# Output projection and ternary network of a two-layer block, made one stage

## The chip, the cores and the metric

The kernel is one program on one core of a Trainium2 chip. Times are device microseconds (us). An execution's time is a little longer than the span that its profile shows, by what lies around the span.

The engines are TensorE (PE in the profile, its weight loads PEld), VectorE (DVE), ScalarE (ACT), GpSimd (POOL) and SyncE (SP), which issues the DMAs. Each runs its own list of instructions in order; between lists only semaphores order the work. PEclk is the TensorE clock that was granted, as a share of its upper level.

## The reference

The input x has 8 x 256 rows of 512 values. Two layers run over it, each an attention and a feed-forward network. The change touches what follows the attention of the second layer: its output projection, and the network with ternary weights.

```python
# L1_xattn, its end: 16 heads of 32, attention weights rounded to 1/255 of each row's largest
out = jnp.einsum('bhqk,bhkd->bhqd', attn, v)
return out @ Wp + bp                      # Wp [512, 512]
...
# L1_ffn
def _bit_quant(w):
    scale = jnp.maximum(jnp.mean(jnp.abs(w)), EPS)
    return jnp.clip(jnp.round(w / scale), -1.0, 1.0)   # the value that is used
w1q = _bit_quant(w1)                      # [2048, 512]
w2q = _bit_quant(w2)                      # [512, 2048]
h = jnp.einsum('bsd,fd->bsf', x, w1q) + b1
h = jax.nn.gelu(h, approximate=False)
return jnp.einsum('bsf,df->bsd', h, w2q) + b2
...
x = x + _L1_xattn_ref(_layernorm(x), ctx, Wq, bq, Wkv, bkv, Wp, bp)
x = x + _L1_ffn_ref(_layernorm(x), w1, b1, w2, b2)
```

The mean of the absolute weights runs over a whole matrix, so no weight can be made ternary before all of its matrix has been read.

## The kernel before

x stays on the chip as 16 tiles of 128 rows (`x_sb`, NT = 16). The program is a row of stages, each a block in which every engine has its list; no engine passes the end of a stage before all have reached it. The stages are: the attention and the gated network of the first layer, keys, values, queries, `attend`, `project` and `ternary_ffn`. The last three matter here.

`attend` goes through 256 units (16 tiles by 16 heads). For each, TensorE makes the scores, ScalarE their exponentials as bytes (L1571), a DMA on SyncE's queue turns the bytes (`a_pairs`, L1443), GpSimd widens them (L1550), and TensorE weighs the values into `a_psO`, which VectorE keeps in `QO` (L1513).

`project` works by tile. VectorE divides by the sum of the exponentials (`p_o`, L1621); TensorE turns the tile (`p_psX`, L1685); ScalarE scales it (`p_oT`, L1659); TensorE multiplies it by Wp in four-byte floats (`p_psY`, L1692); VectorE adds the bias (L1628) and the product (L1633) to x and takes the tile's statistics (L1636). Wp and bp are fetched at the stage's start, and behind them on the same queue w1 and w2 (4 MB each, into `KT`, which the attention no longer needs). In the second half of the stage ScalarE sums the absolute values of w1 and w2, one of 16 pieces at a time (L1669). At the end VectorE works out the normalisation for all 16 tiles (L110 to L112 and a chain of small operations).

`ternary_ffn` first makes w1 ternary as a whole, on VectorE, in three operations of 128 x 8192 (L1785 to L1787). Then it goes through four chunks of 512 rows (NTC = 4, TPC = 4 tiles in each). A chunk is two passes on TensorE. The up pass makes 16 groups (FC = 16) of 128 hidden values by 512 rows: eight products each of 128 x 512, since x is held as two half-precision parts, hi and lo (`t_psH`, L1869). The down pass follows when the whole hidden layer of the chunk is there: per tile 32 products into one bank (`t_psY`, L1881). Between the passes TensorE turns the next chunk's rows (`t_psX`, L1860). ScalarE applies gelu (L1845); VectorE splits its result into hi (L1804) and lo (L1806). In the first chunk VectorE also makes one group of w2 ternary ahead of each split (L1785 to L1787, now 128 x 512). `t_psH` has two buffers and `t_h` two.

There is no scheduler: each engine's order is written out by hand, and chunks 1 and 2 run in a loop of registers.

## Time and profile before

| what | value |
|---|---|
| three runs, median (lowest to highest) | 1968.65 us (1966.84 to 1968.81) |
| the profiled execution | 1971.55 us, of it 1969.8 us span |
| busy, share of the span | PE 89%, DVE 80%, ACT 62%, POOL 47% |
| mean granted clock | 0.958 |
| the attention's last VectorE copy | starts at 1614.71 |
| the first up product of the ternary network | starts at 1714.01 |
| the last addition to x | starts at 1966.41 |

The shares are means over stages with different limits, so the table doesn't say what an edit in one stage is worth. For that the views of the stretch from 1614 us to the end are read: what each engine did, what it waited for, and which wait ended last. A product of 128 x 512 shows a duration of 0.38 us, but the next one starts 0.216 us later: products overlap, and what counts is the distance between their starts. The same holds, less strongly, for VectorE: 0.68 us operations that don't depend on each other start 0.60 us apart.

### The profile page before, as it was taken

To read this page: it belongs to the slowest core of one execution; us is meant where nothing else is said; L and a number is where in the kernel's file an instruction comes from. 1 tells how busy PE (TensorE), PEld (TensorE's weight loads), DVE (VectorE), ACT (ScalarE), POOL (GpSimd) and SP (SyncE) were. 2 spreads that over 40 slices of the span, in tenths; PEclk is the share of its full clock that TensorE was granted. 3 is DMA by queue.
4 is the path that set the end of the run, shared out by engine and by line. 5 is a ranking of instruction groups with operands and counts; after the bars stand their busy time and mean duration, and the time that the engine had idled before them with its cause. 6 is when DMAs were issued, how large, how long until landed. Compare 5 with 4: busy or idle time off the path is not lost. (4 is left out here: it accounts for less than half of the span.)

```text
span 1969.8 us, 32510 instructions
## 1 busy us (share of the span) xinstructions
PE 1760.5 (89%) x11262; PEld 786.4 (40%) x11262; DVE 1584.5 (80%) x2930; ACT 1230.8 (62%) x2011; POOL 918.7 (47%) x935
## 2 busy tenths in 40 slices
PE   4999989599999969939899999999999969579998
PEld 1322322144444435425344444444444434234443
DVE  5899999776776678868899999999999956774433
ACT  4888876455454324414599999999999965222111
POOL 6576764464544300020188888888888850000000
PEclk8999999799999989959899999999999989799999
DMA  9764640300000021000054555555565553000000
GB/s 210 205 163 108 160 119 12 110 11 11 22 0 22 0 80 34 24 27 0 16 108 108 108 108 107 109 106 110 103 109 108 108 131 142 6 6 17 22 22 22
DMA packets 334720, 147.54 MB, mean 75 GB/s; under 512 B 290544, under 2 KB 306928, under 8 KB 333424
## 3 DMA queue, kind: packets, MB, share of 16 engines
q1 hardware_dynamic: 334576, 145.70, 31.8%
q8 instruction: 81, 1.33, 0.3%
q14 instruction: 63, 0.52, 0.1%
HBM read 70.15 MB, written 4.19 MB: 38 GB/s over the span
## 5 line engine op out<-in xcount | busy, mean ns | idle before, releaser
L1571 ACT ACTIVATE a_prob<-a_psS,a_bias,q_scale 128x1024 uint8<-128x1024 f32 x512 | 610.2, 1211 | 28.3 <-PE a_psS L1464 24.4
L1500 DVE TENSOR_REDUCE a_tops<-a_psM 128x1 f32<-128x512 f32 x1024 | 622.6, 677 | 2.2 <-PE a_psM L1454 0.8
L1550 POOL CAST a_wide<-a_pairs 128x2048 int16<-128x2048 uint8 x256 | 481.4, 1891 | 99.5 <-DMA a_pairs<-a_prob 84.8
L1454 PE MATMUL a_psM<-KT,QO 128*128 128x512 bf16 x1024 | 370.7, 387 | 5.6 <-PEq L1248 2.2
L1464 PE MATMUL a_psS<-KT,QO 128*128 128x512 bf16 x1024 | 305.4, 380 | 4.3 <-ACT a_prob L1571 4.3
L1476 PEld LDWEIGHTS a_psO<-V,a_wide 128*128 128x128 f16 x4096 | 175.1, 96 | 146.4 <-DVE QO L1513 23.0
L1476 PE MATMUL a_psO<-V,a_wide 128*128 128x32 bf16 x4096 | 181.5, 177 | 21.8 <-DVE QO L1513 15.6
L854 DVE SCALAR_TENSOR_TENSOR g_sum<-g_psG,gu_scale,g_sum 128x512 f32<-128x512 f32 x176 | 124.2, 745 | 89.7 <-PE g_psG L1006 74.9
L832 POOL TENSOR_TENSOR g_sum<-g_sum 128x512 f32<-128x512 f32 x88 | 126.3, 1436 | 140.4 <-DVE g_sum L854 140.4
L489 ACT ACTIVATE prob<-psT 128x512 f32<-128x512 f32 x256 | 142.9, 598 | 68.5 <-PE psT L698 68.1
L953 ACT ACTIVATE g_sum<-g_psG,gu_scale 128x512 f32<-128x512 f32 x176 | 111.2, 681 | 109.6 <-PE g_psG L1006 108.9
L554 DVE TENSOR_REDUCE rmax<-psS 128x1 f32<-128x512 f32 x256 | 158.6, 673 | 12.1 <-PE psS L684 10.5
L1019 PE MATMUL g_psY<-raw_dn,g_hT 128*128 128x512 f32 x352 | 163.1, 592 | 0.0
L1454 PEld LDWEIGHTS a_psM<-KT,QO 128*128 128x128 bf16 x1024 | 96.9, 96 | 137.4 <-DVE a_tops L1500 133.3
L1845 ACT ACTIVATE t_h<-t_psH,t_b 128x512 f32<-128x512 f32 x64 | 44.0, 687 | 162.3 <-PE t_psH L1869 143.5
L684 PE MATMUL psS<-ks,qs 128*128 128x512 f16 x256 | 93.1, 395 | 41.9 <-POOL qs L413 22.0
L1464 PEld LDWEIGHTS a_psS<-KT,QO 128*128 128x128 bf16 x1024 | 96.4, 98 | 68.7 <-ACT a_prob L1571 12.6
L413 POOL TENSOR_TENSOR qs<-xs,q_sub 128x512 f16<-128x512 f32 x64 | 74.8, 1191 | 87.6 <-ACT q_sub L481 83.3
L1571 ACT ACTIVATION_READ_ACCUMULATOR a_prob<-a_psS,a_bias,q_scale 128x1 f32 x512 | 105.5, 206 | 0.0
L1869 PE MATMUL t_psH<-t_xT_hi,t_w1q 128*128 128x512 f16 x256 | 98.4, 385 | 6.6 <-ACT t_h L1845 5.1
L1881 PE MATMUL t_psY<-t_w2q,t_hT_hi 128*128 128x512 f16 x256 | 99.1, 387 | 2.0 <-DVE t_hT_lo L1806 2.0
L694 PE MATMUL psT<-qs,ks 128*128 128x512 f16 x256 | 98.4, 384 | 0.9 <-ACT prob L489 0.9
(211 smaller groups left out, 2862.0 us busy)
## 6 DMA issues: line engine op xcount, KB each, us to landing
xs<-in_x SPq DMA_DIRECT2D x64, 256.0 KB, 6.5
cs<-in_ctx SPq DMA_DIRECT2D x64, 256.0 KB, 8.4
KT<-in_w SPq DMA_DIRECT2D x2, 4096.0 KB, 21.1
raw_gu<-in_gu SPq DMA_DIRECT2D x4, 1408.0 KB, 8.4
vs<-in_ctxT SPq DMA_DIRECT2D x16, 256.0 KB, 2.8
k_cT<-in_ctxT SPq DMA_DIRECT2D x16, 256.0 KB, 2.7
a_pairs<-a_prob SPq DMA_TRANSPOSE x256, 2.7
out<-x_sb SPq DMA_DIRECT2D x16, 256.0 KB, 2.0
```

The source lines that it names most:

```text
L489: act.activation(prob[:, g % RING, :], psT[g % NT3][:, :], ACT.Exp, scale=float(D0) ** -0.5).then_inc(exped, 1)
L554: v.reduce_max(rmax[j % 2][:, n:n + 1], psS[(NG * j + n) % 3][:, :], AX.X).then_inc(maxed, 1)
L832: pool.tensor_tensor(a[:, :], a[:, :], b[:, :], ALU.add).then_inc(totalled, 1)
L854: v.scalar_tensor_tensor(out=acc[:, :], in0=psG[q % CH][:, :], scalar=gu_scale[:, i * FG + p, g:g + 1], in1=acc[:, :], op0=ALU.mult, op1=A ...
L953: act.activation(part_sum[g][i][m % 3][:, :], psG[q % CH][:, :], ACT.Copy, scale=gu_scale[:, i * FG + p, g:g + 1]).then_inc(scaled, 1)
L1019: mm = pe.matmul(psY[k][:, :], hT[t % 2][:, f, k * P:(k + 1) * P], w_dn[:, f, :], start=(f == 0), stop=(f == FG - 1))
L1454: pe.matmul(psM[n % NM][:, :], QOf[:, i * P:(i + 1) * P], KTf[:, keys:keys + 512], start=True, stop=True).then_inc(shown, 1)
L1464: mm = pe.matmul(psS[g % NS][:, c * 512:(c + 1) * 512], QOf[:, i * P:(i + 1) * P], KTf[:, keys + c * 512:keys + (c + 1) * 512], start=True ...
L1476: mm = pe.matmul(psO[:, h * D1:(h + 1) * D1], wide[i % NV][:, parity, c, :].bitcast(F16), V[:, h, 2 * c + parity, :], start=(parity == 0 a ...
L1500: v.reduce_max(tops[i // JOIN % NB][:, i % JOIN, c:c + 1], psM[n % NM][:, :], AX.X).then_inc(topped, 1)
L1550: pool.tensor_copy(wide[i % NV][:, :, :, :].rearrange("p k c q -> p k (c q)"), both).then_inc(widened, 1)
L1571: act.activation(prob[i % NP][:, k * HK:(k + 1) * HK], psS[g % NS][:, :], ACT.Exp, scale=q_scale[:, i:i + 1], bias=bias[i // JOIN % NB][:, ...
```

## The change

`project` and `ternary_ffn` become one stage, `project_and_ternary`, without a register loop.

- Wp and bp are fetched during `attend`, in five DMAs on SyncE's queue between the turning DMAs of units 112, 128, 144, 160 and 176, into parts of `QO` whose queries have been used.
- The projection has four result banks (`t_psD`) instead of two, and the same order on TensorE.
- The first chunk's rows are normalised, split into hi and lo and turned during the projection. The turning, for all chunks, is done by DMA (`x_turned`) instead of by TensorE: two DMAs of 128 x 2048 per chunk.
- The sums of absolute weights start at tile 5 instead of tile 8. The totals are made at tile 11; from tile 12 VectorE scales and clips two groups of w1 per tile (`clip`, two operations), and ScalarE takes the rounding constant off (`whole`, one operation). Eight groups of w1 are made so before the first up product or beside it (AHEAD = 8); the rest, and all of w2, go group by group through the first chunk.
- In the network, the down products of a group follow three groups behind its up products (LAG = 3). Each group's down products go to all four tiles' banks, two into each. The hidden layer is held for six groups (RING = 6) instead of 16. Up results have four banks, gelu results three buffers.
- The hi part of the hidden layer is made on ScalarE (`high`), the lo part on VectorE (`split`).
- The normalisation of tiles 4 to 15 is worked out on VectorE within group 1 of the first chunk.
- The four tiles of a chunk are finished on VectorE after group 3 of the next.

```diff
@@ attend, SyncE
+            def fetch(c):
+                sp.wait_ge(o_read, CH + 1)
+                if c < CH:
+                    sp.dma_start(spare[:, c, :].bitcast(F32), wp_in[c * P:(c + 1) * P, :]).then_inc(env["wp_loaded"], 16)
+                else:
+                    sp.dma_start(spare[:, c, :].bitcast(F32),
+                                 bp_in.partition_broadcast(P)).then_inc(env["wp_loaded"], 16)
             for i in range(N):
...
+                if i % H1 == 0 and FIRST_LOAD <= i // H1 <= FIRST_LOAD + CH:
+                    fetch(i // H1 - FIRST_LOAD)
@@ project_and_ternary, VectorE
+            def clip(i, f):
+                src = raw[i][:, f]
+                v.tensor_scalar(src, src, inv[:, i:i + 1], -1.0, ALU.mult, ALU.max).then_inc(w_clipped[i], 1)
+                v.wait_ge(w_clipped[i], 2 * f + 1)
+                v.tensor_scalar(src, src, 1.0, ROUND, ALU.min, ALU.add).then_inc(w_clipped[i], 1)
...
+            for t in range(NT):
+                v.tensor_tensor(xt, xt, bp, ALU.add).then_inc(biased, 1)
+                if t + 2 < NT:
+                    divide(t + 2)
+                if t == 4:
+                    v.wait_ge(after_s, TPC)
+                    normalise_tiles(v, env, 0, TPC)
+                if t == 5:
+                    normalise(0, 0)
+                    normalise(0, 1)
+                if t == 7:
+                    for k in (0, 1):
+                        low_part(0, k)
+                        normalise(0, k + 2)
+                if t == 9:
+                    low_part(0, 2)
+                    low_part(0, 3)
+                if t == 11:
+                    v.wait_ge(w_summed, 2 * WS)
+                    v.reduce_sum(sums[:, :], ...).then_inc(summed, 1)
+                if t == 12:
+                    scales(own)
+                if t >= 12:
+                    clip(0, 2 * (t - 12))
+                    clip(0, 2 * (t - 12) + 1)
+                project(t)
+            for t in range(NTC):
+                for p in range(FC):
+                    m = FC * t + p
+                    if t == 0 and AHEAD + p < FC:
+                        clip(0, AHEAD + p)
+                    if t == 0:
+                        clip(1, p)
+                    if m == 1:
+                        v.wait_ge(after_s, NT)
+                        normalise_tiles(v, env, TPC, NT)
+                    split(m)
+                    if t and p == LAG:
+                        for k in range(TPC):
+                            finish(t - 1, k)
...
+            for k in range(TPC):
+                finish(NTC - 1, k)
@@ ScalarE
+            for t in range(NT):
+                scaled(t)
+                if 5 <= t < 5 + WS:
+                    sum_part(2 * (t - 5))
+                    sum_part(2 * (t - 5) + 1)
+                if t == 8:
+                    high_part(0, 0)
+                    high_part(0, 1)
+                if t == 10:
+                    high_part(0, 2)
+                    high_part(0, 3)
+                if t >= 14:
+                    whole(0, 2 * (t - 14))
+                    whole(0, 2 * (t - 14) + 1)
+            for f in range(4, AHEAD):
+                whole(0, f)
+            for t in range(NTC):
+                for p in range(FC):
+                    gelu(m)
+                    high(m)
+                    if t == 0 and AHEAD + p < FC:
+                        whole(0, AHEAD + p)
+                    if t == 0:
+                        whole(1, p)
@@ TensorE
+            def up(t, p):
+                if p == 0:
+                    pe.wait_ge(x_turned[t % 2], 32 * (t // 2 + 1))
+                if t == 0:
+                    pe.wait_ge(w_ready[0], p + 1)
...
+            def down(g):
+                pe.wait_ge(h_split, g + 1)
+                for k in range(TPC):
+                    if f == 0:
+                        pe.wait_ge(added, NT + TPC * (t - 1) + k + 1)
+                    for s in range(2):
+                        mm = pe.matmul(psD[k][:, :], hT[s][:, g % RING, k * P:(k + 1) * P], w2q(f), ...)
+            def due(m):
+                if m % FC == LAG and m > FC:
+                    return []
+                if m % FC == LAG + 1 and m > FC:
+                    return [m - LAG - 1, m - LAG]
+                return [m - LAG] if m >= LAG else []
```

So at each later chunk, TensorE does no down products after up group 3 and those of two groups after up group 4.

**VectorE in the first chunk.** Before, each group of w2 takes three operations, then come the hi and lo parts of the hidden group (`t_h0` is gelu's result):

```order
L1785 TENSOR_SCALAR KT<-KT,t_inv 128x512
L1786 TENSOR_SCALAR KT<-KT 128x512
L1787 TENSOR_SCALAR t_w2q<-KT 128x512
L1804 CAST t_hT_hi<-t_h0 128x512
L1806 TENSOR_TENSOR t_hT_lo<-t_h0,t_hT_hi 128x512
L1769 TENSOR_SCALAR t_xn0<-x_sb,x_mv,x_rstd 128x512
L1769 TENSOR_SCALAR t_xn1<-x_sb,x_mv,x_rstd 128x512
```

After, `KT` with 4x128 is a group of w1, `KT` with 512 one of w2, and `t_hT_lo` the split:

```order
L1738 TENSOR_SCALAR KT<-KT,t_inv 128x4x128
L1740 TENSOR_SCALAR KT<-KT 128x4x128
L1738 TENSOR_SCALAR KT<-KT,t_inv 128x512
L1740 TENSOR_SCALAR KT<-KT 128x512
L1744 TENSOR_TENSOR t_hT_lo<-t_h0,t_hT_hi 128x512
L1738 TENSOR_SCALAR KT<-KT,t_inv 128x4x128
L1740 TENSOR_SCALAR KT<-KT 128x4x128
L1738 TENSOR_SCALAR KT<-KT,t_inv 128x512
L1740 TENSOR_SCALAR KT<-KT 128x512
L111 BN_AGGR x_mv<-x_stats 128x2 x12
L113 TENSOR_SCALAR norm_ve<-x_mv 128x12
```

Two of five operations of a group have gone to ScalarE, one more group of w1 has come in, and the normalisation of twelve tiles stands ahead of the second split.

**VectorE in the projection.** Before, from the addition of one tile's product (`p_psY0`) to that of the next, a turn is four operations:

```order
L1633 TENSOR_TENSOR x_sb<-x_sb,p_psY0 128x512
L1636 BN_STATS x_stats<-x_sb 128x6
L1628 TENSOR_TENSOR x_sb<-x_sb,p_bias 128x512
L1621 TENSOR_TENSOR p_o1<-QO,p_inv 128x512
L1633 TENSOR_TENSOR x_sb<-x_sb,p_psY1 128x512
```

After, the turn of tile 7 (`V` holds the hi and lo parts of x, `t_h0` and `t_h1` the normalised rows):

```order
L1764 TENSOR_TENSOR x_sb<-x_sb,QO 128x512
L1706 TENSOR_TENSOR t_o1<-QO,e_sum 128x512
L1729 TENSOR_TENSOR V<-t_h0,V 128x512
L1723 TENSOR_SCALAR t_h0<-x_sb,x_mv,x_rstd 128x512
L1729 TENSOR_TENSOR V<-t_h1,V 128x512
L1723 TENSOR_SCALAR t_h1<-x_sb,x_mv,x_rstd 128x512
L1713 TENSOR_TENSOR x_sb<-x_sb,t_psD3 128x512
L1715 BN_STATS x_stats<-x_sb 128x6
```

Between the division of tile 9 and the addition of tile 7 four operations have come in.

**TensorE, from the up to the down products.** Before, at the end of the first up pass:

```order
L1869 MATMUL t_psH1<-t_xT_hi,t_w1q 128x512
L1869 MATMUL t_psH1<-t_xT_lo,t_w1q 128x512
L1860 MATMUL t_psX0<-id_f,t_xn0 128x128 x4
L1860 MATMUL t_psX1<-id_f,t_xn1 128x128 x4
L1860 MATMUL t_psX0<-id_f,t_xn2 128x128 x4
L1860 MATMUL t_psX1<-id_f,t_xn3 128x128 x4
L1881 MATMUL t_psY0<-t_w2q,t_hT_hi 128x512
L1881 MATMUL t_psY0<-t_w2q,t_hT_lo 128x512
```

After, around up group 3 of the first chunk (`QO` holds the ternary weights, `V` the turned rows):

```order
L1927 MATMUL t_psU2<-V,QO 128x512 x8
L1927 MATMUL t_psU3<-V,QO 128x512 x8
L1940 MATMUL t_psD0<-QO,t_hT_hi 128x512
L1940 MATMUL t_psD0<-QO,t_hT_lo 128x512
L1940 MATMUL t_psD1<-QO,t_hT_hi 128x512
L1940 MATMUL t_psD1<-QO,t_hT_lo 128x512
L1940 MATMUL t_psD2<-QO,t_hT_hi 128x512
L1940 MATMUL t_psD2<-QO,t_hT_lo 128x512
L1940 MATMUL t_psD3<-QO,t_hT_hi 128x512
L1940 MATMUL t_psD3<-QO,t_hT_lo 128x512
L1927 MATMUL t_psU0<-V,QO 128x512 x8
```

The turnings have left TensorE, and the down products of group 0 stand between the up products of groups 3 and 4.

## Rows read from the trace of the kernel before

**Rows 1.** Stretches of the end: busy us per engine, granted clock, DMA share.

```profile
1615.00:1623.00 8.00, 0.37 (x2) 0.38 (x3) 4.57 (x7) 0.00 (x0) 0.00 (x0) 0.50 0.73 232
...
1687.00:1714.00 27.00, 4.49 (x18) 3.65 (x19) 23.53 (x48) 3.23 (x5) 0.00 (x0) 0.58 0.03 11
1714.00:1760.00 46.00, 34.26 (x146) 15.21 (x147) 39.89 (x87) 13.25 (x21) 0.00 (x0) 0.91 0.00 1
1760.00:1967.00 207.00, 200.77 (x928) 91.62 (x926) 83.46 (x146) 37.67 (x57) 0.00 (x0) 0.98 0.05 19
```

**Rows 2.** Timeline 1614 to 1634: start, us, engine, line, what, [idle before].

```profile
1614.71 0.69 DVE L1513 COPY QO<-a_psO 128x512 f32<-128x512 f32 x1 [17.70 <-PE a_psO L1476]
...
1616.11 0.50 SPq L1610 DMA_DIRECT2D p_bias<-in_bp  x1
...
1622.63 1.97 PE L1685 MATMUL p_psX<-id_f,p_o 128*128 128x128 f32 x8 [7.95 <-DMA p_bias<-in_bp]
...
1624.97 4.34 PE L1692 MATMUL p_psY<-p_w,p_oT 128*128 128x512 f32 x8 [0.38 <-ACT p_oT L1659]
```

**Rows 3.** Timeline, VectorE adding the projection, two turns.

```profile
1652.66 0.69 DVE L1633 TENSOR_TENSOR x_sb<-x_sb,p_psY 128x512 f32 x1 [1.06 <-PE p_psY L1692]
...
1656.54 0.69 DVE L1633 TENSOR_TENSOR x_sb<-x_sb,p_psY 128x512 f32 x1 [1.06 <-PE p_psY L1692]
```

**Rows 4.** Timeline, last projection tile to first up product.

```profile
1687.07 0.69 DVE L1633 TENSOR_TENSOR x_sb<-x_sb,p_psY 128x512 f32<-128x512 f32 x1 [1.42 <-PE p_psY L1692]
...
1688.52 1.17 DVE L110 BATCH_NORM_AGGREGATE x_mv<-x_stats 128x2 f32<-128x6 f32 x16
...
1692.64 0.17 DVE L93 TENSOR_TENSOR x_rstd<-x_rstd,norm_tmp 128x16 f32<-128x16 f32 x1
...
1696.42 4.49 DVE L1785 TENSOR_SCALAR KT<-KT,t_inv 128x8192 f32<-128x8192 f32 x1
...
1714.01 0.58 PE L1869 MATMUL t_psH<-t_xT_hi,t_w1q 128*128 128x512 f16 x1 [1.50 <-DVE t_xT_lo L1793]
```

**Rows 5.** Chain that ended last, 1750 to 1970: start, us, what.

```profile
1759.73 29.22 PE t_psY L1881 x128
1788.95 27.64 PE t_psH L1869 x128
...
1820.46 27.63 PE t_psY L1881 x128
...
1966.41 0.69 DVE x_sb L1819
```

**Rows 6.** Groups by line and shape, 1615 to 1970 | busy us, mean ns.

```profile
L1806 DVE TENSOR_TENSOR t_hT_lo<-t_h,t_hT_hi 128x512 f16<-128x512 f32 x64 | 44.3, 692 | 2.2
L1845 ACT ACTIVATE t_h<-t_psH,t_b 128x512 f32<-128x512 f32 x64 | 44.0, 687 | 162.3 <-PE t_psH L1869 143.5 <-DVE t_hT_lo L1806 18.7
...
L1669 ACT ACTIVATE p_junk<-KT 128x1024 bf16 x12 | 12.8, 1064 | 1.3 <-ACT p_junk L1669 1.3
...
L1785 DVE TENSOR_SCALAR KT<-KT,t_inv 128x512 f32<-128x512 f32 x16 | 7.7, 480 | 0.0
...
L1669 ACT ACTIVATION_READ_ACCUMULATOR p_junk<-KT x12 | 2.4, 202 | 0.0
```

**Rows 7.** The same view, gated network, 480 to 700.

```profile
L941 ACT ACTIVATE g_half_hi<-g_xn 128x512 f16<-128x512 f32 x8 | 5.0, 630 | 20.8 <-DVE g_xn L844 20.8
```

**Rows 8.** Two stretches of the gated network, as rows 1.

```profile
384.00:388.00 4.00, 1.12 (x4) 0.13 (x2) 3.55 (x15) 1.66 (x3) 0.00 (x0) 0.50 0.00 0
400.00:680.00 280.00, 278.25 (x957) 121.09 (x956) 198.60 (x308) 139.37 (x245) 136.82 (x100) 1.00 0.05 12
```

**Rows 9.** DMA issues of the gated network; last, median us to landing.

```profile
g_xT_lo<-g_half_lo SPq DMA_TRANSPOSE x2, 4.1
```

**Rows 10.** The same for the whole program (part 6 of the page).

```profile
KT<-in_w SPq DMA_DIRECT2D x2, 4096.0 KB, 21.1
```

**Rows 11.** Waits in the attention: who <- whom: total us, times, longest.

```profile
ACT a_prob L1571 <- DMA a_pairs<-a_prob: 3.4, 6, 1.0
```

More of the change, by code:

```diff
@@ L1402, in attend @@
     AHEAD, LAG, JOIN = 4, 4, 2
+    FIRST_LOAD = 7
     OW = P // 2
@@ L1625, in turn, with invert @@
[L1625 to L1630 removed]
+            def invert(own, first, end):
+                part = sums_of[:, first * H1:end * H1, :]
+                own.link(v.tensor_tensor(part[:, :, 0], part[:, :, 0], part[:, :, 1], ALU.add))
+                own.link(v.tensor_scalar(part[:, :, 0], part[:, :, 0], SUBNORMAL, None, ALU.mult))
+                own.link(v.reciprocal(part[:, :, 0], part[:, :, 0]))
```

490 lines of the change are left out of this document (231 added, 259 removed).

## The prediction

> **What bounds the kernel now.** I read the stretches first. Up to 1615 us nothing is changed but five small DMAs, so the question is what TensorE does in the 355 us from there to the end. It is busy all but 6 us of the last 207, but only 4.5 of the 27 us from 1687 to 1714 and 34 of the next 46, at a granted clock of 0.58 and 0.91 [rows 1]. Then the timeline: the stage of the projection begins with TensorE and VectorE waiting for the bias, issued at 1616.11 and there at 1622.63 [rows 2]. In the projection TensorE sets the pace: VectorE's additions come 3.88 us apart and VectorE is idle for 1.06 us before each [rows 3]. After the last tile comes a chain on VectorE, normalisation, then w1 made ternary as a whole, and the first up product starts at 1714.01 [rows 4]. The first up pass goes at VectorE's pace: 39.9 us busy of 46 [rows 1]. The chain that ended last then shows TensorE alone: passes of 128 products in 27.64 us, which is 0.216 us a product, and about 3.9 us between an up and a down pass, in which the last group's gelu, its split and the turning of rows are waited for [rows 5]. So three things cost time: a start, a 27 us hole, and passes that wait for their neighbours.
>
> **The sum, in the times of the profiled execution.**
>
> Start. Wp and bp are there already. VectorE begins at about 1615.7 as before; it inverts two tiles' sums (three small operations, an estimated 0.6 us together from the 0.2 us spacing of the small chain in [rows 4]) and divides tile 0 (0.69), so TensorE starts at 1617.0. From its first turning to its first projection product it took 2.34 us [rows 2]; I keep that, and the slow clock with it (PEclk 0.50 in this stretch, [rows 1]). 1619.4 instead of 1624.97: 5.6 us won. The bounds are 4 and 7.
>
> Projection. TensorE's work is the same, 62.1 us from 1624.97 to 1687.07 [rows 2, 4]. VectorE gets more: about 3.4 us of normalisation at tile 4 (the 16-tile chain took 4.3, [rows 4], of which 1.17 falls to a quarter), four normalised tiles at 0.48 and four low parts at 0.69 [rows 6], sixteen clips at 0.48 [rows 6], 0.6 for the scales: 16.4 us, against 16 turns with 1.06 idle each [rows 3]. It just fits as a sum, but comes in lumps, and TensorE can run only about one turn ahead of the divisions. The lump at tiles 4 and 5 is 4.4 us against 2.1 of idle and a little over a microsecond of lead: about 1 us of stall. At tile 7 VectorE also waits for a high part, which stands on ScalarE's list behind tile 8's scaling and two sums (1.27 each, [rows 6]): about 2.3 us. The same at tile 9: about 1.3. The clips of tiles 12 to 15 cost 1.9 us a turn against 1.06 idle, and from tile 14 the division is gone: 1. Near 6 us lost; the bounds are 0 (the lead absorbs it) and 8. The sums start at tile 5, some 23 us after the weights are asked for, and those land in 21.1 us in the median of the two [rows 10]; w1 is the first, and w2 is needed only at tile 9. I cost that at nothing.
>
> The hole. Up group 0 needs four things: the turned rows, the first ternary group, b1 and a free bank. The low parts are ready by tile 10, the two turning DMAs land some 4.1 us after each issue [rows 9], and five tiles of 3.88 cover them; the first group's last operation is ScalarE's, at tile 14, with a turn and a half of cover. So the up products follow the last projection product: 27.0 us won (1687.07 to 1714.01, [rows 4]). Bounds 24 and 27.
>
> First chunk. Before, from 1714.01 to the next chunk's first up product at 1788.95: 74.9 us [rows 4, 5]. After: 256 products at 0.216 are 55.3 us if TensorE is never late. VectorE enters the chunk about 2.8 us after TensorE. Then, with operations of 0.48 and 0.69 [rows 6]: addition and statistics 1.4, four clips 1.9, split 0.7; then four clips 1.9, twelve tiles' normalisation 4.1 (from the 4.3 of [rows 4]), split 0.7: the second split ends about 13.5 us into the chunk. TensorE wants it after five ups and one down, 10.4 us in. A stall of 3 us, and 0.5 for the first w2 group. A stall of that size brought the clock to 0.50 in the gated network [rows 8]; an estimated 1 us for that. 59.8 us: 15.1 won; bounds 10 and 19. From group 3 on a group needs 3.46 us of TensorE, at most 4 x 0.48 + 0.69 = 2.6 of VectorE, and 0.69 + 3 x 0.63 = 2.6 of ScalarE [rows 6, 7] (`whole` isn't in the trace; I take it like the copy of [rows 7]. The ends are 0.48, like a clip, and 1.27, like a sum; at 1.27 ScalarE needs 3.9 us a group, 0.4 more than TensorE, 3 us over eight groups.) So TensorE sets the pace there.
>
> Chunks 1 to 3. Before 177.5 us (1788.95 to 1966.41, [rows 5]). After, three times 55.3, and at each chunk's group 3 a new wait: the down products of the new chunk may not touch a bank before the old tile has been added to x. Split 3 is done 0.69 + 0.63 + 0.69 us after up group 3 [rows 6, 7], the first addition 0.69 later: 2.8 us with the gaps, while up group 4 covers 1.73. That is 1.2, and each of the next three additions (0.69) is 0.27 late against a pair of products (0.43). 2.0 us per chunk; queued behind it on TensorE is everything. 171.9: 5.6 won; bounds 0 and 9.
>
> End. Four additions come after the last products instead of one; the first can start 1.3 us before TensorE ends: 0.7 lost.
>
> Attention. Five more DMAs share the queue of the turning DMAs. ScalarE waited for those DMAs only 3.4 us in 256 units [rows 11]. Such a fetch took 6.5 us behind another one [rows 2]; fully exposed, five would cost 32. The units have three buffers, so I take 0.5; bounds 0 and 32.
>
> Sum: 5.6 - 6.0 + 27.0 + 15.1 + 5.6 - 0.7 - 0.5 = 46.1 us won. The profiled execution took 1971.55; the median of the runs is 1968.65, and the difference goes over unchanged: **1968.65 - 46.1 = 1922.5, say 1922 us.**
>
> **A rule on the down products.** In the gated network TensorE goes through four up banks and four down banks in just this manner, and there it is busy 278.3 of 280 us at a clock of 1.00 [rows 8]. The Trainium skill, page "TensorE: Matmul & The Clock Gate", section "A second HAM failure mode: psum-queue depth-cycling", says that going through banks in each iteration leaves small gaps between groups, that the clock then swings between its two levels, and that throughput suffers. By that rule the network's products would not all run at 2.4 GHz; it is rival D below. The trace of the gated network speaks against it.
>
> **A rule on the clips.** A contiguous clip of 512 values took 0.48 us and a two-operand operation of that size 0.69 [rows 6]; the new view of w1 is four pieces of 128. The Trainium skill, page "VectorE: DVE Perf Modes", section "What auto-detection actually checks", says that one source in SBUF keeps the double rate when the outermost dimensions are even; by that rule 0.48 stays and rival B falls away. No trace here shows it for this view.
>
> **Rivals.**
>
> B, the pieces of w1 are slow: each of the 32 w1 operations takes 0.69. Sixteen fall on VectorE in tiles 12 to 15, where it has no idle time left, 3.4 us, and four before the second split, 0.8; the late start adds some: 5 us, 1927. For it: nothing in the trace has that shape. Against it: nothing either, but the pieces are whole.
>
> C, the lumps are absorbed: TensorE's lead is longer than the turn I give it, the 6 and 3 us of stalls go to 1 and 0, and the time is 1914. For it: VectorE's work fits into its idle time as a sum [rows 3]. Against it: the second split comes late by a count of operations.
>
> D, slower than before: stalls of a microsecond or two recur, and the clock stays down, as in the gated network's first chunk (0.50 from 384 to 388, [rows 8]). The network's 512 up and 512 down products are 221 us at the upper level; the 46 us are used up when they take 267, a mean clock of 0.83. At 0.75 they take 295: 1996. For it: the early stretch of the gated network, where VectorE was just as loaded. Against it: it recovered within 20 us.
>
> E, the fetches are felt: the turning DMAs behind them come late, and the attention is bound by a chain with little slack. At a third of the exposure, 10 us: 1933. If w2's sums were late as well, the change would not do what it says, and w1 would again be waited for; the 5 tiles of cover speak against that.
>
> **Chances.** Forecast 0.70, B 0.11, C 0.09, E 0.06, D 0.04. The forecast's own range is 1917 to 1928. The range for 8 in 10 takes in C and B and most of E's near side: 1913 to 1933. A change of under 0.2% (4 us) can't be told from none here. Faster by more than that 0.95, within it 0.01, slower 0.04.
>
> **What would show it.** Right: the first projection product at about 1619; the first up product within 2 us of the last projection product, near 1687; VectorE before TensorE in the waits of tiles 7 to 12; one stall of about 3 us at the second group of down products; three of about 2 us with the addition to x as releaser; PEclk 1.00 from 1710 on; TensorE's last product near 1919. Wrong: clips of 0.69; a mean distance of products over 0.22 us in chunks 1 to 3; ScalarE's exponentials waiting for the DMA in tiles 7 to 11; or up group 0 waiting for the turned rows.

## The result, and the profile after

| | before | after |
|---|---|---|
| median of the runs, us | 1968.62 | 1919.05 |
| lowest to highest | 1966.84 to 1968.81 | 1913.82 to 1924.04 |
| profiled execution: time, span | 1971.55, 1969.8 | 1915.59, 1913.8 |
| start of the attention's last keep | 1614.7 | 1610.5 |
| first up product | 1714.0 | 1682.0 |
| A: last keep to first up product | 99.3 | 71.5 |
| B: first up product to the end of the span | 255.8 | 231.8 |

The ratio of the times is 0.975, with a 95% interval of 0.9718 to 0.9782. The forecast was 1922 (1913 to 1933); the result is 3 us below it. A keep is VectorE's copy of an attention result into `QO`. A and B are the two parts of what was changed; together they went from 355.1 to 303.3 us. They are used for every run below, since the end of the unchanged stages ahead of them, the last keep, moves by 10 us from one profile to the next (1607.7 to 1617.8 in the table of the experiments).

The stretches of the kernel after (the columns as in [rows 1]), which answer to [rows 1]:

```profile
1615.00:1623.00 8.00, 7.56 (x19) 3.56 (x19) 4.53 (x7) 2.71 (x11) 0.00 (x0) 0.81 1.02 431
1623.00:1687.00 64.00, 60.86 (x193) 28.99 (x192) 51.97 (x108) 42.41 (x100) 0.00 (x0) 1.00 0.28 88
1687.00:1714.00 27.00, 25.72 (x120) 11.52 (x119) 24.42 (x72) 21.86 (x36) 0.00 (x0) 1.00 0.00 1
1714.00:1760.00 46.00, 44.87 (x207) 19.79 (x206) 21.80 (x41) 23.76 (x37) 0.00 (x0) 1.00 0.19 46
1760.00:1912.00 152.00, 147.55 (x679) 65.51 (x676) 50.71 (x81) 57.71 (x89) 0.00 (x0) 1.00 0.13 33
```

Where TensorE was busy 4.5 us of 27 it is now busy 25.7, and its granted clock is 1.00 in every stretch from 1623 on. All its waits for another engine in the stage (from 1612 to 1914; total, times, longest) are four groups:

```profile
PE t_psU L1901 <- DVE t_o L1706: 5.9, 4, 2.7
PE t_psD L1940 <- DVE x_sb L1755: 3.4, 3, 1.1
PE t_psD L1940 <- DVE t_hT_lo L1744: 1.3, 1, 1.3
PE t_psD L1909 <- ACT t_hT_hi L1821: 0.4, 1, 0.4
```

The first group is the start (2.7) and three stalls in the projection (0.96 at 1640.8, 1.67 at 1654.3, 0.51 at 1662.8); the second is the three chunk boundaries; the third is the second down group of the first chunk.

The timeline at the start, which answers to [rows 2]:

```profile
1610.53 0.69 DVE L1531 COPY QO<-a_psO 128x512 f32<-128x512 f32 x1 [17.16 <-PE a_psO L1494]
1611.54 0.19 DVE L1698 TENSOR_TENSOR e_sum<-e_sum 128x32 f32<-128x32 f32 x1 [0.32 <-PEq L1411]
1613.20 1.94 PE L1901 MATMUL t_psU<-id_f,t_o 128*128 128x128 f32 x8 [2.72 <-DVE t_o L1706]
1615.59 1.22 PE L1909 MATMUL t_psD<-QO,t_hT_hi 128*128 128x512 f32 x1 [0.44 <-ACT t_hT_hi L1821]
```

The first projection product comes 5.06 us behind the last keep instead of 10.26.

The timeline of TensorE where the hole was [rows 4]:

```profile
1679.46 2.74 PE L1909 MATMUL t_psD<-QO,t_hT_hi 128*128 128x512 f32 x6
1682.04 7.07 PE L1927 MATMUL t_psU<-V,QO 128*128 128x512 f16 x32
...
1690.67 1.89 PE L1927 MATMUL t_psU<-V,QO 128*128 128x512 f16 x8
1693.84 0.39 PE L1940 MATMUL t_psD<-QO,t_hT_hi 128*128 128x512 f16 x1 [1.28 <-DVE t_hT_lo L1744]
```

The last projection products run straight into 32 up products; the one stall is 1.28 us.

The timeline at a chunk boundary, and behind it two groups of the chain that ended last (they answer to [rows 5]):

```profile
1747.23 0.69 DVE L1744 TENSOR_TENSOR t_hT_lo<-t_h,t_hT_hi 128x512 f16<-128x512 f32 x1 [2.76 <-ACT t_hT_hi L1860]
1747.84 2.48 DVE L1755 TENSOR_TENSOR x_sb<-t_psD,x_sb 128x512 f32<-128x512 f32 x4
1748.67 0.38 PE L1940 MATMUL t_psD<-QO,t_hT_hi 128*128 128x512 f16 x1 [1.13 <-DVE x_sb L1755]
1749.18 0.39 PE L1940 MATMUL t_psD<-QO,t_hT_hi 128*128 128x512 f16 x1
1749.78 0.39 PE L1940 MATMUL t_psD<-QO,t_hT_hi 128*128 128x512 f16 x1
```

```profile
1748.67 4.04 PE t_psD L1940 x16
...
1805.64 4.04 PE t_psD L1940 x16
...
1862.61 4.04 PE t_psD L1940 x16
1902.90 6.92 PE t_psD L1940 x32
```

VectorE takes the split first, then the four additions 0.60 us apart; TensorE waits 1.13 us and then goes at the additions' pace. The period of a chunk is 56.97 us, so the boundary costs 1.7 us over 55.3 of products.

The operations of the stage from 1682 on, by line (x count, busy us, mean ns, idle before), beside [rows 6, 7]:

```profile
L1744 DVE TENSOR_TENSOR t_hT_lo<-t_h,t_hT_hi 128x512 f16<-128x512 f32 x64 | 44.2, 691 | 123.3 <-ACT t_hT_hi L1860 123.3
L1860 ACT ACTIVATE t_hT_hi<-t_h 128x512 f16<-128x512 f32 x64 | 40.3, 629 | 2.1
L1841 ACT ACTIVATE QO<-KT,t_less_round 128x512 f16<-128x512 f32 x26 | 17.8, 709 | 5.8 <-DVE KT L1740 5.6
L1738 DVE TENSOR_SCALAR KT<-KT,t_inv 128x512 f32<-128x512 f32 x25 | 12.0, 480 | 0.0
```

VectorE now waits 123 us for ScalarE's high parts in B. It sets nothing there but for the first groups.

### The profile page after: what moved, and what is told of

It is laid out like the page before. It is cut to its first block and busy times, and to the rows that moved or that the text cites. A ratio compares the mean times of both kernels' runs of the same rounds, so it can differ in the third digit from the quotient of the medians.

```text
span 1913.8 us, 31933 instructions
## 1 busy us (share of the span) xinstructions
PE 1724.0 (90%) x11054; PEld 775.2 (41%) x11198; DVE 1547.2 (81%) x2897; ACT 1291.2 (67%) x2107; POOL 921.4 (48%) x936
## 5 line engine op out<-in xcount | busy, mean ns | idle before, releaser
L1472 PE MATMUL a_psM<-KT,QO 128*128 128x512 bf16 x968 | 352.1, 385 | 18.3 <-DVE a_tops L1518 12.6
L1482 PE MATMUL a_psS<-KT,QO 128*128 128x512 bf16 x967 | 293.3, 380 | 6.6 <-ACT a_prob L1589 3.6
L560 DVE TENSOR_REDUCE rmax<-psS 128x1 f32<-128x512 f32 x256 | 158.9, 676 | 12.7 <-PE psS L690 10.6
L1744 DVE TENSOR_TENSOR t_hT_lo<-t_h,t_hT_hi 128x512 f16<-128x512 f32 x64 | 44.2, 691 | 123.3 <-ACT t_hT_hi L1860 123.3
L1849 ACT ACTIVATE t_h<-t_psU,t_b 128x512 f32<-128x512 f32 x64 | 43.7, 682 | 92.7 <-PE t_psU L1927 92.7
L1940 PE MATMUL t_psD<-QO,t_hT_hi 128*128 128x512 f16 x256 | 97.1, 379 | 4.7 <-DVE x_sb L1755 3.4
```

The costliest lines, as they stand in the source:

```text
L560: v.reduce_max(rmax[j % 2][:, n:n + 1], psS[(NG * j + n) % 3][:, :], AX.X).then_inc(maxed, 1)
L1472: pe.matmul(psM[n % NM][:, :], QOf[:, i * P:(i + 1) * P], KTf[:, keys:keys + 512], start=True, stop=True).then_inc(shown, 1)
L1482: mm = pe.matmul(psS[g % NS][:, c * 512:(c + 1) * 512], QOf[:, i * P:(i + 1) * P], KTf[:, keys + c * 512:keys + (c + 1) * 512], start=True ...
L1940: mm = pe.matmul(psD[k][:, :], hT[s][:, g % RING, k * P:(k + 1) * P], w2q(f), start=(f == 0 and s == 0), stop=(f == FC - 1 and s == 1))
```

## The experiments

Each row is one profile; the base is the changed kernel, profiled twice. "Against" is the sum A + B against the mean of the two, 303.8 us. The last column is measured over all runs against the kernel before.

| run | last keep | A | B | A + B | against | ratio to before, 95% |
|---|---|---|---|---|---|---|
| changed | 1610.5 | 71.5 | 231.8 | 303.3 | | 0.9750 (0.9718 to 0.9782) |
| changed, again | 1614.1 | 72.5 | 231.8 | 304.3 | | 0.9742 (0.9729 to 0.9755) |
| additions ahead | 1617.2 | 70.9 | 226.7 | 297.5 | -6.2 | 0.9707 (0.9694 to 0.9721) |
| normalisation later | 1617.8 | 71.0 | 230.3 | 301.3 | -2.5 | 0.9729 (0.9716 to 0.9742) |
| low parts later | 1609.2 | 69.6 | 231.8 | 301.4 | -2.3 | 0.9722 (0.9709 to 0.9735) |
| the three together | 1612.4 | 69.8 | 225.2 | 295.0 | -8.8 | 0.9695 (0.9669 to 0.9721) |
| Wp fetched in the stage | 1613.4 | 77.5 | 231.8 | 309.3 | +5.5 | 0.9760 (0.9744 to 0.9777) |
| x turned behind the projection | 1608.4 | 86.4 | 233.4 | 319.8 | +16.0 | 0.9816 (0.9800 to 0.9833) |
| w1 quantised behind it | 1614.8 | 74.6 | 233.0 | 307.5 | +3.8 | 0.9765 (0.9749 to 0.9781) |
| one group behind | 1607.7 | 71.2 | 235.8 | 307.0 | +3.2 | 0.9768 (0.9752 to 0.9784) |
| blocks of seven | 1611.0 | 71.1 | 233.9 | 305.0 | +1.2 | 0.9738 (0.9716 to 0.9761) |
| VectorE's share | 1617.1 | 70.9 | 236.5 | 307.4 | +3.6 | 0.9756 (0.9740 to 0.9772) |
| both of these | 1610.2 | 72.4 | 241.9 | 314.4 | +10.6 | 0.9788 (0.9772 to 0.9804) |

B is repeated to 0.1 us where nothing in it was touched (231.8 in four profiles). A is not: eight profiles with the same projection (both of the changed kernel, additions ahead, normalisation later, and the last four rows) lie between 70.9 and 72.5. All of that lies in one place, the first tile's eight projection products. These are two of the eight profiles, the changed kernel again and the additions ahead:

```profile
1619.19 5.92 PE L1909 MATMUL t_psD<-QO,t_hT_hi 128*128 128x512 f32 x8 [0.44 <-ACT t_hT_hi L1821]
```

```profile
1622.23 4.28 PE L1909 MATMUL t_psD<-QO,t_hT_hi 128*128 128x512 f32 x8 [0.44 <-ACT t_hT_hi L1821]
```

In their first 4.3 us the granted clock was 0.50 and 0.86. Without these products A is 66.6 us in each of the eight (66.59 to 66.62). So a difference in B, and one in A without the first tile, is read to a few tenths; one in A as it stands in the table only to about 2 us. Idle times of TensorE are a little short as prices: a wait also ends the overlap of two products, which start 0.216 us apart while one lasts 0.38, so it costs some 0.16 more than its idle time.

**The changed kernel again.** No edit.

> The changed kernel once more, nothing altered. It is the base for the other three runs of this group and tells where the 10 us between its own runs (1913.8 to 1924.0) come from. Theory U (the spread lies in the unchanged stages ahead): the new stage, from the last keep of the attention to the end of the span, takes 303.3 us within 1 us again, whatever the total. Rival S (it lies in the new stage, a clock that falls or waits that differ): the total and that stretch move together, by up to 10 us. Ratio to the kernel before 0.972 to 0.978 in either case.

Theory U held: 304.3 against 303.3 us, and the 1.0 is the first tile's products (5.92 against 4.90). The 10 us arise ahead of the change. In two profiles the first product of the gated network, 1250 us before the stage, is apart by 4.8 us already, first the changed kernel's, then that of the run with the normalisation later:

```profile
L1012 PE MATMUL g_psG<-first_xT_hi,w_gu x176: 379/379/634, 362.3 to 597.4; 128*128 128x512 f16 x176
```

```profile
L1012 PE MATMUL g_psG<-first_xT_hi,w_gu x176: 379/379/634, 367.1 to 603.6; 128*128 128x512 f16 x176
```

Of the 56.0 us between the two spans, 51.8 are therefore the change (50.8 by the second profile) and 4.2 such differences.

**Additions ahead of the split.**

```diff
+ if t and p == LAG:
+     for k in range(TPC):
+         finish(t - 1, k)
  split(m)
- if t and p == LAG:
-     for k in range(TPC):
-         finish(t - 1, k)
```

> The four additions to x of the previous chunk stand ahead of the split of group 3 instead of behind it, in chunks 1 to 3. Theory: the pauses of TensorE at the three boundaries (1.13 us idle and then four pairs 0.60 apart instead of 0.43, together 1.7 us each) are only the additions' place behind the split, so 4 to 5 us go (0.9975 of the changed kernel), the period of a chunk falls from 56.97 to 55.4 us. Rival 1: the split of group 3 now comes 2.4 us late and the wait moves to it or to ScalarE's ring of three: 0 to 1 us. Rival 2: the pairs at 0.60 come from the bank being read and written in turn, whatever the order: only the 1.1 goes, 3.4 us in all.

B is 5.1 us shorter, 1.7 a boundary, and of the waits of B only the first chunk's 1.3 is left. The timeline of this run at the first boundary:

```profile
1750.41 2.48 DVE L1755 TENSOR_TENSOR x_sb<-t_psD,x_sb 128x512 f32<-128x512 f32 x4
1753.25 0.69 DVE L1744 TENSOR_TENSOR t_hT_lo<-t_h,t_hT_hi 128x512 f16<-128x512 f32 x1 [0.37 <-ACT t_hT_hi L1860]
...
1749.94 3.62 PE L1927 MATMUL t_psU<-KT,QO 128*128 128x512 f16 x16
1753.39 0.38 PE L1940 MATMUL t_psD<-QO,t_hT_hi 128*128 128x512 f16 x1
```

The additions lie beside up groups 3 and 4, and even the split doesn't suffer: it waits 0.37 us for ScalarE behind them. Both rivals fall.

**Normalisation of 12 tiles later.**

```diff
- if m == 1:
-     v.wait_ge(after_s, NT)
-     normalise_tiles(v, env, TPC, NT)
  split(m)
...
+ if m == 3:
+     v.wait_ge(after_s, NT)
+     normalise_tiles(v, env, TPC, NT)
```

> The normalisation of the 12 remaining tiles (4.0 us of small operations of VectorE) stands behind the split of group 3 instead of ahead of the split of group 1. Theory: the 1.28 us that TensorE waits at the second down group go, and no new wait comes, since by then the group being split is three ahead of the one that TensorE multiplies: 1.3 us (0.9993). Rival 1: the clips of w2 for groups 1 to 3 are late anyway, and half of it stays. Rival 2: behind group 3 the 4 us make VectorE late for group 4 or 5, and the stall comes back there: 0 or slightly slower, up to 2 us.

B is 1.5 us shorter, 1.28 of idle time and the 0.16 of a wait, and the wait for `t_hT_lo` is gone; nothing came in its place. As the theory had it.

**Low parts one tile later.**

```diff
- if t == 7:
+ if t == 8:
      for k in (0, 1):
          low_part(0, k)
          normalise(0, k + 2)
- if t == 9:
+ if t == 10:
      low_part(0, 2)
      low_part(0, 3)
```

> In the projection the two places at which VectorE takes the low parts of the first chunk (tiles 7 and 9) stand one tile later (8 and 10). Theory: VectorE stands there for ScalarE's high parts, and TensorE behind it for 1.67 and 0.51 us; one tile later the high parts are ready, and 1.5 to 2.2 us go (0.999). Rival 1: it is not the wait but the work, VectorE being full there (51.97 of 64 us busy): the stalls move to tiles 8 and 10 at the same size, 0 us. Rival 2: the first turning starts 4 us later and the first up product waits: slower; it would need over 25 us of delay, so this I hold for excluded.

The waits for `t_o` are now 3.7 us in two times, instead of 5.9 in four: those of 1.67 and 0.51 are gone, and no new one is there. A is 69.6, 1.2 below the lowest of the eight, and without the first tile's products (5.51) it is 64.1 instead of 66.6: 2.5 us, a little more than the 2.2 of idle time.

**The three together.**

> The three moves that each shortened the new stage, in one kernel: the additions to x ahead of the split of group 3, the small operations of the 12 tiles behind it, the low parts of the first chunk a tile later. Theory: they remove three different waits (5.1, 1.3 and 2.2 us), so they add up: 8.5 us less in the stage (from the last keep to the end 295 us against 303.3 and 304.3), ratio to the kernel before 0.9700. Rival: they share one cause, VectorE's backlog, and together bring no more than the largest alone, 5 to 6 us: stage 298, ratio 0.9713.

295.0 us as expected, and B is 231.8 - 5.1 - 1.5 = 225.2 to the tenth. A without the first tile's products is 64.1, as with the low parts alone. Three waits with a cause each; the rival falls. What is left of TensorE's waits in the stage:

```profile
PE t_psU L1901 <- DVE t_o L1706: 3.7, 2, 2.7
PE t_psD L1909 <- ACT t_hT_hi L1821: 0.4, 1, 0.4
```

This kernel beats both: 0.9695 of the time before, about 9 us under the changed kernel.

**Wp and its bias fetched at the head of the stage.** The first two lines are the attention's.

```diff
- if i % H1 == 0 and FIRST_LOAD <= i // H1 <= FIRST_LOAD + CH:
-     fetch(i // H1 - FIRST_LOAD)
...
+ for c in range(CH):
+     sp.dma_start(spare[:, c, :].bitcast(F32), wp_in[c * P:(c + 1) * P, :]).then_inc(w_in, 16)
+ sp.dma_start(spare[:, CH, :].bitcast(F32), bp_in.partition_broadcast(P)).then_inc(w_in, 16)
```

> The five transfers of Wp and its bias go back from the attention to the head of the new stage; all else as in the changed kernel. Theory: the first projection product comes 10 us after the last keep again instead of 5.0, since it waits for the bias as in the kernel before [rows 2]: 4.5 to 6 us slower than the changed kernel, 1.0026 of it. Rival 1: in the attention they cost something that comes back (the attention takes 591.0 us in the profiles of the changed kernel, 591.6 before): then less than 4 us. Rival 2: five transfers in a row instead of two take longer to issue: 7 to 8 us slower.

A is 77.5, 5.5 us over the mean of the two, and 6.0 without the first tile's products (B is unchanged). The first projection product comes 11.1 us behind the last keep, 0.85 later than in the kernel before. Whether that is the five transfers instead of two wasn't taken apart; rival 2's 7 to 8 us in all it is not. The wait for the bias is back:

```profile
PE t_psU L1894 <- DMA QO<-in_bp: 8.7, 1, 8.7
```

The attention gives nothing back that can be told: from its first keep to its last it takes 590.2 us in this run, 590.2 to 591.7 in the twelve profiles with the fetches in it, 591.6 before. ScalarE's exponentials waited 2.3 us for the turning DMAs in the changed kernel, 1.1 to 3.3 in the others with the fetches, 2.0 in this run and 3.4 before [rows 11].

**The first chunk's x turned behind the projection.** All of it stands behind the last tile, on ScalarE the four high parts too.

```diff
- if t == 4:
-     v.wait_ge(after_s, TPC)
-     normalise_tiles(v, env, 0, TPC)
- if t == 5:
-     normalise(0, 0)
-     normalise(0, 1)
...
  project(t)
+ v.wait_ge(after_s, TPC)
+ normalise_tiles(v, env, 0, TPC)
+ normalise(0, 0); normalise(0, 1)
+ for k in (0, 1):
+     low_part(0, k); normalise(0, k + 2)
+ low_part(0, 2); low_part(0, 3)
```

> The normalisation, the splitting into parts and the turning of the first chunk stand behind the projection's 16 tiles, as in the kernel before; the first eight groups of w1 are still quantised in the projection. It takes the hole of 27 us apart. Theory: the chain of x is back on the path by itself: small operations 3.5 us, four tiles through two buffers 4, the turning 4.6, together 12 to 13 us until the first up product, and 1 to 3 us for a clock that fell meanwhile: 13 to 16 us slower than the changed kernel (1.0075 of it). Rival: weights were what the 27 us hung on, and x's chain was mostly under them: under 6 us. Second rival: the clock stays at its lower level for 10 us of work: over 20 us.

The hole is 17.64 us, more than I had expected of x's chain alone. The timeline of this run:

```profile
1678.05 0.68 DVE L1713 TENSOR_TENSOR x_sb<-x_sb,t_psD 128x512 f32<-128x512 f32 x1
...
1682.76 1.00 DVE L1723 TENSOR_SCALAR t_h<-x_sb,x_mv,x_rstd 128x512 f32<-128x512 f32 x2
...
1686.37 1.47 DVE L1729 TENSOR_TENSOR V<-t_h,V 128x512 f16<-128x512 f32 x2
...
1687.93 4.41 SPq L1671 DMA_TRANSPOSE V<-V  x2
...
1694.78 8.55 PE L1919 MATMUL t_psU<-V,QO 128*128 128x512 f16 x28 [17.64 <-issue]
```

Addition and small operations 4.7 us, parts 5.2, and from the turning's issue to the first up product 6.9 (I had reckoned 4.6). The projection behind its first tile is 3.8 us shorter (57.9 against 61.7), without the stalls and with VectorE less full. The granted clock is 0.83 from 1694 to 1710 and 1.00 behind that, so the second rival falls, and the first too: x's chain makes a hole of 17.6 us by itself.

**w1 quantised behind the projection.** Four groups behind the last tile, and ScalarE's roundings of them there too.

```diff
- LAG, RING, AHEAD = 3, 6, 8
+ LAG, RING, AHEAD = 3, 6, 4
- if t >= 12:
-     clip(0, 2 * (t - 12))
-     clip(0, 2 * (t - 12) + 1)
  project(t)
+ for f in range(AHEAD):
+     clip(0, f)
```

> None of w1's groups is quantised in the projection: four are behind its last tile, the other twelve in the first chunk, one with each group (so 12 instead of 8 there). Theory: the first up product waits for an addition, a bn_stats, two clips and one rounding, 3 to 3.5 us, and ScalarE does four roundings (2.8 us) before the first gelu, which makes the first down groups late by as much again: 5 to 7 us slower than the changed kernel (1.003). Rival 1: the first chunk is full and can't take four more groups on VectorE (1.9 us of clips and 0.6 of a split against 3.46 us of TensorE a group): 10 us and more. Rival 2: clips in the projection delayed the additions to x there as much as they save later: 0 to 2 us.

The waits, from the timeline of this run:

```profile
1688.47 3.30 ACT L1840 ACTIVATE QO<-KT,t_less_round 128x512 f16<-128x512 f32 x4 [8.10 <-DVE KT L1740]
1689.34 3.12 PE L1923 MATMUL t_psU<-V,QO 128*128 128x512 f16 x8 [3.27 <-ACT QO L1840]
```

3.3 us of wait, as expected, and 1.2 more in B, where the first eight products took 3.12 us instead of 1.9. The backlog of roundings on ScalarE, which I had added to it, lay mostly under that wait. 3.8 us in all, or 4.6 without the first tile's products (3.4 in A, 1.2 in B), below the 5 that I gave as the least; the direction and the place were right. Rival 1 (a full first chunk) falls. So does rival 2: the projection behind its first tile takes 61.7 us with the clips and without them.

**One group behind instead of three.**

```diff
- LAG, RING, AHEAD = 3, 6, 8
+ LAG, RING, AHEAD = 1, 6, 8
```

> The down products run one group behind the up products instead of three (a ring of six as before). Theory: in the steady part one group is enough, since gelu 0.68, high part 0.63 and split 0.6 take 2.1 us with what lies between and there are 3.46 us until the products that need them; only the first chunk loses, where the 4.0 us of small operations and the first clips of w2 stand ahead of the first splits: 3 to 5 us slower than the changed kernel (1.002). Rival: every group's products wait for their split, 0.3 to 0.5 us each, 64 times: 20 to 30 us slower, and the clock falls with it.

B is 4.0 us longer; the waits for a split went from 1.3 us to 5.0: 2.4 and 2.2 in the first chunk, and 0.4 for the last group of all. In between one group of lag is as good as three (56.97 us a chunk in both), and the rival falls.

**Blocks of seven in the first chunk.**

```diff
- LAG, RING, AHEAD = 3, 6, 8
+ LAG, RING, AHEAD = 3, 7, 8
  def due(m):
+     if m < FC + LAG:
+         return {6: list(range(7)), 13: list(range(7, 14)), 15: [14, 15]}.get(m, [])
```

> In the first chunk the down products come in blocks behind the up products: groups 0 to 6 behind up 6, 7 to 13 behind up 13, 14 and 15 behind up 15 (a ring of seven for the hidden parts instead of six); the other chunks as in the changed kernel. It takes back, as far as the memory allows, the mixing of the two kinds of product in the first chunk. Theory: there ScalarE has 2.7 us a group to do (two roundings of 0.71, gelu 0.68, high part 0.63) against 1.73 us of an up product alone, and 3.46 of an up and a down product; so seven up products in a row wait for ScalarE by about 1 us each, twice, and the last groups for their split: 10 to 14 us slower than the changed kernel (1.006). Rival: the first chunk gained by work that went to the projection (eight groups of w1, the chunk's own x), not by the mixing: 0 to 4 us.

My theory fell: B is 2.1 us longer, not 10 to 14, and inside the rival's 0 to 4. TensorE meets no wait in seven groups of up products in a row; its waits are in the down products, 2.6 us in all. What follows is my reading, since no run changes the number of buffers: with four banks and three buffers of gelu TensorE can run ahead of ScalarE for seven groups, and ScalarE catches up during the block of down products. I had taken ScalarE's rate for the pace of a block.

**VectorE's share back.** The rounding stands behind each pair of clips, the high part at the head of `split`; ScalarE's three lines go.

```diff
+ v.tensor_scalar(dst, raw[i][:, f], ROUND, None, ALU.subtract).then_inc(w_ready[i], 1)
...
+ v.tensor_copy(hT[0][:, m % RING, :], h[m % 3][:, :]).then_inc(h_hi, 1)
  v.wait_ge(h_hi, m + 1)
...
- high(m)
- whole(0, AHEAD + p)
- whole(1, p)
```

> The high parts of the hidden values (all chunks) and the roundings of the first chunk go back from ScalarE to VectorE, as in the kernel before; order of the products, lag and all else as in the changed kernel. Theory: in the first chunk VectorE then needs 3.87 us a group while there are four clips, two roundings (0.43), a high part (0.42) and a low part (0.69), against TensorE's 3.46, and 2.45 us in the last eight groups; eight times 0.41 and the backlog that it enters the chunk with: 4 to 7 us slower than the changed kernel (1.003). So ScalarE's share is worth about a third of the 15 us won in the first chunk. Rival: the division between the two engines is all of it, and these 15 us are lost again: 12 to 16 us slower. Second rival: the mixed order covers it: 0 to 2 us.

B is 4.7 us longer, within the 4 to 7 expected; both rivals fall. The waits for a split are 4.7 us in two times, the longer 3.5, and the eight products behind that one come some 0.42 us apart instead of 0.22.

**Both.** The two edits above together.

> Both at once: VectorE takes the high parts and roundings, and the first chunk's down products come in blocks of seven, seven and two. It is the nearest to the first chunk of the kernel before that the memory allows. Theory: with VectorE full the mixing matters, since its work for seven groups (27 us) can't be done ahead of seven up products in a row: 3 to 6 us on top of the run with VectorE's share alone. Rival, from the run in blocks alone (1 to 2 us lost, where I had expected 10 to 14): the total of VectorE's work sets the time in either order, and the blocks cost 0 to 2 us on top.

B is 10.1 us longer than in the changed kernel, 5.4 more than with VectorE's share alone. The waits for a split, in the order of the last three runs (in blocks alone the releaser is mostly a rounding of w2):

```profile
PE t_psD L1940 <- ACT QO L1841: 2.2, 3, 1.2
PE t_psD L1940 <- DVE t_hT_lo L1744: 0.4, 1, 0.4
```

```profile
PE t_psD L1950 <- DVE t_hT_lo L1757: 4.7, 2, 3.5
```

```profile
PE t_psD L1950 <- DVE t_hT_lo L1757: 10.8, 7, 2.3
```

So blocks alone cost 2.1, VectorE's share alone 4.7, and both 10.1: against blocks of seven the mixed order is worth 2 us while ScalarE carries its part and 5.4 while VectorE carries it all.

## Why the prediction came out right, step by step

| step | forecast, won | measured, won |
|---|---|---|
| start | 5.6 | 5.2 |
| projection and hole | -6.0 + 27.0 | 22.6 |
| first chunk | 15.1 | 18.1 |
| chunks 1 to 3 | 5.6 | 6.5 |
| end | -0.7 | -0.6 |
| attention | -0.5 | +0.5 |

The measured rows are worked out thus. Start: 10.26 - 5.06. Projection and hole: from the first projection product to the first up product 89.0 us before [rows 2, 4], 66.45 after (1615.59 to 1682.04). First chunk: 74.9 before [rows 4, 5]; after, chunk 1's first up product is at 1733.6, with three groups of down products (5.2) still due: 56.8. Chunks 1 to 3: 177.5 before; after from 1738.8 to 1909.8, the end of the last group in the chain: 171.0. The end: 4.0 against 3.4. Attention: 591.6 - 591.1.

**Start.** Right, and shown by taking it back (6.0 us). Rival E falls with it: what the fetches cost the attention is less than the 1.5 us by which it differs from profile to profile, and so is the 0.5 in the table.

**Projection.** Direction and places were right: stalls at tiles 4/5, 7 and 9, with VectorE's division as the releaser. I had 1 + 2.3 + 1.3 and found 0.96 + 1.67 + 0.51; that they hang on the place of the low parts is shown by the run with these later. The fourth stall, 1 us at tiles 12 to 15, did not come. Instead the first tile's eight products took 4.90 us against 4.34 before [rows 2] (the second tile's took 3.60): TensorE starts them in a stretch at a mean clock of 0.81. It differs from one profile to the next with nothing changed in it, 4.28 to 5.92 in the eight named above. Stalls and start make 3.7 of the 4.35 us by which the projection is longer; the rest is what each wait costs beyond its idle time, and 0.3 in the turn with the product of the sums (L1915), whose turnings lie 4.15 us apart instead of 3.87.

**Hole.** Right: no gap at all between the last projection product and the first up product. It is shown in two parts, each put back by itself: x's chain (17.6) and w1's first groups (3.3, with four instead of the whole of w1). They are not terms of a sum, since in the kernel before VectorE did both one after the other. The sums' turn and the quantisation of w1 as a whole are in the trace of before [rows 4] and were not put back.

**First chunk.** The one stall was at the place that I named, the second group of down products, but 1.28 us long instead of 3, and with no cost for the clock and none for w2's first group. What I had wrong is when VectorE enters the chunk. I had put it at 2.8 us behind TensorE, without a working; its last addition of the projection starts 1.2 us behind the first up product at 1682.04:

```profile
1683.21 0.68 DVE L1713 TENSOR_TENSOR x_sb<-x_sb,t_psD 128x512 f32<-128x512 f32 x1
```

From there to the end of the second split its list takes 10.6 us, against 10.7 in my sum: the overlap of independent operations saves some, a wait of 0.42 for the first high part takes it back. It enters earlier because the backlog that I expected of tiles 12 to 15, as the fourth stall above, did not build up; how much of that is the overlap no run takes apart. The clock term rests on a misread row: in the gated network the product at 384.00, ahead of the wait of 2.88 us that falls into [rows 8], already took 0.63 us, so that wait did not bring the clock down. The shorter stall (1.7), the clock (1.0) and w2 (0.5) make up the 3 us between 15.1 and 18.1. `whole`, for which I had no row, took 0.71, near the price that I took. The two things that I had not taken apart in this term were the mixed order and ScalarE's share. With both taken back the first up product of chunk 2 comes 10.6 us later, of the 18.1 (B is only 10.1 longer, since the two later chunks are 0.2 shorter each). The remaining 7.5 I can't assign by a run. One candidate is the turning of x, which TensorE did between the passes and which is now a DMA; the waits of before from 1712 to 1792 have this row:

```profile
PE t_psX L1860 <- DVE t_xT_lo L1793: 6.7, 1, 6.7
```

Another is a block of 16 groups instead of seven; it wasn't tried. For it speaks the trace of before: there VectorE has no pause from 1718 us to 1757 and the splits (L1806) start 2.38 us apart, so 16 groups take 38 us of VectorE against 27.6 of TensorE, and the wait above stands at the end of that list. In a mixed order the same list has 55.3 us.

**Boundaries.** The new wait was there, three times, with the addition to x as its releaser: 1.13 and then 0.6 a pair, 1.7 in all against 2.0. It hangs on one place in VectorE's order, as the run with the additions ahead shows.

**The rivals.** B: the clips of w1 in four pieces of 128 took 470 to 486 ns, as those of w2 in one piece [rows 6], and the rival falls. By the Trainium skill, page "VectorE: DVE Perf Modes", section "What auto-detection actually checks", the double rate stays for such a view, with one source, source and destination in SBUF, and even outermost dimensions. The trace agrees with its 481 ns. C was nearer than I gave it: with stalls of 3.1 and 1.3 instead of 6 and 3 the result lies between it and the forecast. D: 64 groups go through four up banks and four down banks at a granted clock of 1.00 from 1687 to 1912. The Trainium skill, page "TensorE: Matmul & The Clock Gate", section "A second HAM failure mode: psum-queue depth-cycling", tells of a kernel whose clock swings because going through banks leaves small gaps between its groups of products. This trace has four gaps in its 64 groups (one of 1.28 us, three of 1.13) and no swing: 1.00 in each stretch.

**The level.** The profile of after fell on a short execution of the unchanged part (its last keep 4.2 us earlier than before's), which has nothing to do with the change. Over the medians the gain is 49.6 us, in the stage 51.8 and 50.8; the forecast was 46.1, 46.6 of it in the stage. So the stage gained 4 to 5 us more than forecast, most of it in the first chunk, and the medians of whole runs show 1 to 2 us less of that.

## What to carry to other kernels

When a stage's bound engine stands still while the next stage's weights and rows are prepared, put the preparation into the idle time of the engines of the stage before, in pieces, and check each piece's place: three lists of operations, moved by one or two places, were worth 9 us more here. A wait at a boundary is often the order on the releasing engine, not its load; look at what stands ahead of the releasing operation. And before blaming a slower engine for the pace of a block, count the buffers in front of it: here seven groups of up products in a row, with four banks and three buffers, met no wait.

## What the runs showed of the hardware that I had not expected

The clock stayed up through one stall and fell in others. After 1.28 us at the second down group the next eight products took 1.90 us; after 3.27 us (w1 quantised behind the projection) the first eight took 3.12, and behind the 3.54 us in the run with VectorE's share single products took 0.61 to 0.63 us instead of 0.38. The length of the stall alone doesn't tell: behind 2.38 us in the run with one group behind all eight products took 0.38, but in the gated network before, behind a wait of 2.43 us that ended at 375.64, products took 0.63 from 377.16 to 380. The granted clock (the column behind the busy times) around the first two, of the changed kernel and of that with w1 behind:

```profile
1690.00:1700.00 10.00, 8.72 (x41) 3.81 (x40) 9.28 (x30) 6.72 (x12) 0.00 (x0) 1.00 0.00 1
```

```profile
1688.00:1694.00 6.00, 4.66 (x14) 1.79 (x15) 4.54 (x11) 4.32 (x6) 0.00 (x0) 0.72 0.01 3
```

I had added 1 us for the clock to a stall that then cost the clock nothing. And the state in which the clock is found at the start of the projection is worth up to 1.6 us: the same eight products took 4.28 us at 0.86 and 5.92 at 0.50.

VectorE overlaps independent operations of its list. A clip of another group starts 0.34 us after the start of one of 0.43, an addition 0.60 after one of 0.69; the second clip of a pair, which waits for the first by a semaphore, starts 0.52 after it, and that one lasts 0.48. The four clips of a group's two halves take 1.72 us instead of 1.82, and the four additions of a boundary 2.48 instead of 2.72, so such a list is better priced by the distances of starts than by durations.

The first product of the gated network starts between 359.8 and 369.6 us in the thirteen profiles of after and the experiments, whose code up to there is one and the same. That is more than the best kernel gained over the changed one; only the sums A and B made the smaller experiments readable.
